# The KAN stage of a two-layer network: coefficients stationary, basis moving, output turned back by transposes

## The reference

```python
def _fourier_kan(v, coef):
    vf = v.reshape(-1, shp[-1])
    k = jnp.arange(1, GRID + 1, dtype=v.dtype)          # GRID = 8
    arg = vf[:, :, None] * k
    y = jnp.einsum('nik,jik->nj', jnp.cos(arg), coef[0]) + jnp.einsum('nik,jik->nj', jnp.sin(arg), coef[1])
```

## Time and profile before

| | us |
|---|---|
| median of three runs | 3789.62 |
| lowest, highest | 3781.47, 3795.3 |
| the profiled execution, its own time | 3786.26 |
| its span | 3784.4 |
| KAN, first xn to last statistics | 3331.21 to 3597.51 |

### The profile page before, as it was taken

One profiled execution on the slowest core, in us unless ns is written; L12 is line 12 of the kernel. 1 busy time (PEld: TensorE's weight loads), 2 busy tenths in 40 slices (PEclk: granted clock), 3 DMA queues, 4 the chain that ended last, 5 costly groups with the idle time before them and its releaser, 6 DMA issues. The chain is left out here.

```text
span 3784.4 us, 60070 instructions
## 1 busy us (share of the span) xinstructions
PE 2852.5 (75%) x18634; PEld 2068.5 (55%) x18635; DVE 2710.5 (72%) x4018; ACT 2218.7 (59%) x3974; POOL 2006.3 (53%) x1364
## 2 busy tenths in 40 slices
PE   3899999621799990378888888888888887669934
PEld 2455555321566660146666666666666666569934
DVE  3788788443344446539999999998999999867643
ACT  1566566420233330178899888898989888522242
POOL 1011111166222220169999989898989999512234
PEclk6999999655899995689999999999999999889955
DMA  3444444321111116112222222222222222120050
GB/s 95 92 89 87 83 88 90 103 73 43 39 39 39 39 34 175 30 54 74 77 80 74 78 73 73 75 77 77 77 74 77 77 80 77 58 75 25 16 156 15
DMA packets 220447, 270.13 MB, mean 71 GB/s; under 512 B 36941, under 2 KB 139879, under 8 KB 215323
## 3 DMA queue, kind: packets, MB, share of 16 engines
q1 hardware_dynamic: 199874, 247.61, 25.3%
q0 software_dynamic: 12256, 18.82, 1.5%
q10 hardware_dynamic: 8064, 0.55, 0.2%
HBM read 219.79 MB, written 54.22 MB: 72 GB/s over the span
## 5 line engine op out<-in xcount | busy, mean ns | idle before, releaser
L1740 POOL TENSOR_TENSOR resid_x<-s_ux,s_B_rows 128x1024 f32<-128x1024 f32 x256 | 605.1, 2364 | 144.1 <-PE s_y L2100 143.8
L2020 DVE TENSOR_TENSOR_SCAN resid_x<-s_dA,resid_x 128x1024 f32<-128x1024 f32 x256 | 581.6, 2272 | 127.0 <-ACT s_dA L1831 123.3
L2028 DVE TENSOR_TENSOR_SCAN resid_x<-s_back_decay,s_back_in 128x1024 f32<-128x1024 f32 x256 | 583.9, 2281 | 55.2 <-ACT s_back_decay L1841 55.2
L2100 PE MATMUL s_y<-identity,resid_x 128*128 128x128 f32 x4096 | 556.7, 281 | 18.3 <-issue 11.7
L2100 PEld LDWEIGHTS s_y<-identity,resid_x 128*128 128x128 f32 x4096 | 496.2, 146 | 71.0 <-issue 41.6
L1748 POOL TENSOR_TENSOR resid_x<-resid_x,s_C_rows 128x1024 f32<-128x1024 f32 x192 | 454.4, 2366 | 7.5 <-DVE resid_x L2020 7.5
L2087 PE MATMUL s_back_in<-identity,resid_x 128*128 128x128 f32 x2048 | 294.0, 290 | 139.4 <-ACT resid_x L1852 70.5
L467 DVE TENSOR_REDUCE a_row_max<-a_maxscores 128x2 f32<-128x512 f32 x512 | 336.0, 683 | 80.5 <-PE a_maxscores L545 80.1
L2035 DVE TENSOR_TENSOR resid_x<-resid_x,s_C 128x1024 f32<-128x1024 f32 x320 | 383.0, 1197 | 14.2 <-PE s_C L2077 10.9
L1831 ACT ACTIVATE s_dA<-s_dt,s_A 128x510 f32<-128x510 f32 x512 | 330.0, 675 | 96.3 <-DVE resid_x L2020 96.1
L1852 ACT ACTIVATE resid_x<-s_uT,s_bT 128x256 f32<-128x256 f32 x864 | 368.9, 498 | 1.3
(11 more groups left out here) (333 smaller groups left out, 5618.8 us busy)
## 6 DMA issues: line engine op xcount, KB each, us to landing
s_B_rows<-forward_rows SPq DMA_DIRECT2D x256, 256.0 KB, 3.3
s_C_rows<-forward_rows SPq DMA_DIRECT2D x192, 256.0 KB, 3.3
a_Q<-split_qk SPq DMA_DIRECT2D x96, 192.0 KB
split_qk<-a_parts SPq DMA_DIRECT2D x32, 384.0 KB, 2.8
e_x<-slot_inputs SPq DMA_DIRECT2D x135, 65.0 KB
a_K<-split_qk SPq DMA_DIRECT2D x64, 128.0 KB
f_mod_rows<-mod_rows SPq DMA_DIRECT2D x16, 512.0 KB, 9.7
c_y<-choice_outputs SPq DMA_DIRECT2D x16, 512.0 KB, 6.4
```

The source lines that it names most:

```text
L1740: tt(R[s, 0], ux[par][:], brow[s % BRING][:].unsqueeze(1).broadcast_to([P, C2, W]), ALU.mult).then_inc(S["in_ready"], 1)
L2020: nc.vector.tensor_tensor_scan(r, a, r, 0.0, ALU.mult, ALU.add).then_inc(S["scanned"], 1)
L2028: nc.vector.tensor_tensor_scan(r[:, ::-1], a[:, ::-1], b[:, ::-1], 0.0, ALU.mult, ALU.add).then_inc(S["scanned"], 1)
L2100: last = mm(YP[:, t, c2 * P:(c2 + 1) * P], R[s, d][:, c2, t * P:(t + 1) * P], core.ident[:], is_transpose=True, start=((s, d) == (0, 1) an ...
```

## The change

- The matmul is turned round. WT is stationary and the basis moves as 512 columns: 16 matmuls a group (32 instructions of 512 columns) in place of 64 (128 of 128). The output then has features on partitions. ScalarE copies it from PSUM to SBUF (`yT`), and TensorE turns it back with four transposes into a new PSUM tile `psZ`, called z below, which y1 reads.
- The nine terms that don't need ES (EARLY) are multiplied first, behind a wait for DS and EE; the seven E products (LATE) follow, behind a wait for ES. The transposes of the input of group i+1 stand between.
- xn moves from VectorE to ScalarE, with two buffers, and two groups ahead. D and E move from VectorE to ScalarE, with constants 2 and -2 as bias columns; the squares have two buffers of their own.
- The order on VectorE in turn i is now: rounding and angle of i, ES of i-1, S2 of i, y1 of i-2, DS of i, statistics of i-3.
- The hardware loops are gone: all turns of all five engines are written out. od and gate have one semaphore for each buffer.

```diff
 VectorE (constants two and minus_two are set first)
+                for i in range(NG + 4):
+                    bs, before = basis[i % 2], basis[(i + 1) % 2]
+                    if live(i):
                         dve.wait_ge(S["f_ready"], i + 1)
                         ts(whole[:], f[:], MAGIC, MAGIC, ALU.add, ALU.subtract).then_inc(S["rounded"], 1)
                         dve.wait_ge(S["rounded"], i + 1)
+                        at(dve, S["cos_done"], i)
                         tt(t[:], f[:], whole[:], ALU.subtract).then_inc(S["reduced"], 1)
+                    if live(i, 1):
+                        dve.wait_ge(S["E_ready"], i)
+                        dve.wait_ge(S["D_products"], i)
+                        tt(before[:, B_ES1:B_EDS2 + 1, :], before[:, B_S1:B_DS2 + 1, :], before[:, B_E, :].unsqueeze(1).broadcast_to([P, 7, W4]), ALU.mult)\
+                            .then_inc(S["E_products"], 1)
+                    if live(i):
                         dve.wait_ge(S["cos_done"], i + 1)
                         tt(bs[:, B_S2, :], bs[:, B_S1, :], bs[:, B_C1, :], ALU.mult).then_inc(S["s2_done"], 1)
+                    if live(i, 2):
+                        j = i - 2
+                        dve.wait_ge(S["z_ps"], j + 1)
+                        dve.wait_ge(S["hb_ready"], j + 1)
+                        at(dve, S["gated"], j)
+                        tt(y1[:], psZ[:], hb[:], ALU.add).then_inc(S["y1_ready"], 1)
+                    if live(i):
+                        dve.wait_ge(S["D_ready"], i + 1)
                         dve.wait_ge(S["s2_done"], i + 1)
                         tt(bs[:, B_DS1:B_DS2 + 1, :], bs[:, B_S1:B_S2 + 1, :], bs[:, B_D, :].unsqueeze(1).broadcast_to([P, 3, W4]), ALU.mult)\
                             .then_inc(S["D_products"], 1)
+                    if live(i, 3):
...
+                            last = tile_stats(core, X, j * KT + k)
 ScalarE
+                normed(0)
+                normed(1)
+                turns(0)
+                for i in range(NG + 2):
+                    bs = basis[i % 2]
+                    if live(i):
                         act.wait_ge(S["reduced"], i + 1)
                         at(act, S["products"], i - 1)
                         func(bs[:, B_S1, :], t[:], ACT.Sin, scale=TURN).then_inc(S["sin_done"], 1)
...
+                    if live(i, 2):
+                        j = i - 2
+                        act.wait_ge(S["products"], j + 1)
+                        at(act, S["z_ps"], j)
+                        func(yT[:], psY[:, j % 2, :], ACT.Copy).then_inc(S["yT_ready"], 1)
+                    if live(i):
                         act.wait_ge(S["sin_done"], i + 1)
+                        func(s_square[:], bs[:, B_S1, :], ACT.Square, scale=float(np.sqrt(2))).then_inc(S["q_ready"], 1)
+                        act.wait_ge(S["q_ready"], i + 1)
+                        func(bs[:, B_D, :], s_square[:], ACT.Identity, scale=-2.0, bias=two[:, 0:1]).then_inc(S["D_ready"], 1)
...
+                        func(bs[:, B_E, :], d_square[:], ACT.Identity, bias=minus_two[:, 0:1]).then_inc(S["E_ready"], 1)
...
+                    if live(i + 1):
+                        turns(i + 1)
+                    if live(i + 2):
+                        normed(i + 2)
 TensorE
+                transposes(0)
+                for i in range(NG + 2):
+                    j = i - 1
+                    product = lambda m: nc.tensor.matmul(psY[:, j % 2, :], WT[:, m, :], basis[j % 2][:, m, :], start=(m == EARLY[0]), stop=(m == LATE[-1]))
                     if live(i, 1):
+                        pe.wait_ge(S["D_products"], j + 1)
+                        pe.wait_ge(S["E_square"], j + 1)
+                        at(pe, S["yT_ready"], j - 1)
+                        for m in EARLY:
+                            product(m)
+                    if live(i + 1):
+                        transposes(i + 1)
+                    if live(i, 1):
                         pe.wait_ge(S["E_products"], j + 1)
+                        for m in LATE:
+                            last = product(m)
+                        last.then_inc(S["products"], 1)
+                    if live(i, 2):
+                        n = i - 2
+                        pe.wait_ge(S["yT_ready"], n + 1)
+                        at(pe, S["y1_ready"], n)
                         for k in range(KT):
+                            last = nc.tensor.transpose(psZ[:, k * P:(k + 1) * P], yT[:, k * P:(k + 1) * P], core.ident[:])
+                        last.then_inc(S["z_ps"], 1)
```

More of the change, by code:

```diff
@@ L2322, in kan @@
     NG, W4 = NT // KT, KT * P
-    live = lambda i, lag: not isinstance(i, int) or 0 <= i - lag < NG
+    live = lambda i, lag=0: 0 <= i - lag < NG
     on = ExitStack()
@@ L2339, in kan @@
         psY = core.psum("k_psY", [P, 2, W4], on=on)
+        psZ = core.psum("k_psZ", [P, W4], on=on)
         S = {n: core.sem("k_" + n) for n in (
-            "ln_loaded", "ln_ready", "od_loaded", "gate_loaded", "xn_ready", "xT_ps", "f_ready", "rounded", "reduced", "sin_done", "abs_done",
-            "cos_done", "q_ready", "s2_done", "D_ready", "D_products", "D_square", "E_ready", "E_products", "E_square",
-            "products", "hb_ready", "y1_ready", "gated", "x_updated", "stats", "passed")}
+            "ln_loaded", "ln_ready", "od_loaded0", "od_loaded1", "gate_loaded0", "gate_loaded1", "xn_ready", "xT_ps", "f_ready", "rounded", "reduced",
+            "sin_done", "abs_done", "cos_done", "q_ready", "s2_done", "D_ready", "D_products", "D_square", "E_ready", "E_products", "E_square",
+            "products", "yT_ready", "z_ps", "hb_ready", "y1_ready", "gated", "x_updated", "stats")}
+        EARLY = [m for m in range(NBASIS) if not B_ES1 <= m <= B_EDS2]
+        LATE = list(range(B_ES1, B_EDS2 + 1))
         with nc.Block() as block:
@@ L2365, in _ @@
                 nc.vector.memset(quarter[:], float(np.pi / 2))
+                nc.vector.memset(two[:], 2.0)
+                nc.vector.memset(minus_two[:], -2.0)
                 dve.wait_ge(S["ln_loaded"], 32)
                 ts(ln[:], ln[:], float(1 / (2 * np.pi)), None, ALU.mult).then_inc(S["ln_ready"], 1)
[L2369 to L2393, removed]
+                for i in range(NG + 4):
+                    bs, before = basis[i % 2], basis[(i + 1) % 2]
+                    if live(i):
                         dve.wait_ge(S["f_ready"], i + 1)
@@ L2408, in emit @@
[L2408 to L2413, removed]
+                    if live(i, 3):
+                        j = i - 3
+                        dve.wait_ge(S["x_updated"], j + 1)
+                        for k in range(KT):
+                            last = tile_stats(core, X, j * KT + k)
+                        last.then_inc(S["stats"], 1)
@@ L2419, in _, with normed, turns @@
                 act.wait_ge(S["ln_ready"], 1)
[L2421 to L2426, removed]
+                def normed(i):
+                    act.wait_ge(S[f"od_loaded{i % 2}"], 16 * (i // 2 + 1))
+                    at(act, S["xT_ps"], i - 1)
+                    for k in range(KT):
+                        c = i * KT + k
+                        last = func(xn[i % 2][:, k, :], od[i % 2][:, k, :], ACT.Identity, scale=core.rstd[:, c:c + 1], bias=core.nmr[:, c:c + 1])
+                    last.then_inc(S["xn_ready"], 1)
+                def turns(i):
+                    act.wait_ge(S["xT_ps"], i + 1)
+                    at(act, S["reduced"], i)
+                    func(f[:], psT[:], ACT.Identity, scale=ln[:, 0:1], bias=ln[:, 1:2]).then_inc(S["f_ready"], 1)
+                normed(0)
[4 more added lines that the diff above has]
+                    if live(i):
                         act.wait_ge(S["reduced"], i + 1)
```

72 lines of the change are left out of this document (23 added, 49 removed).

## The result

| | before | changed |
|---|---|---|
| median of four runs, us | 3791.49 | 3816.94 |
| lowest, highest | 3781.47, 3795.3 | 3813.32, 3826.05 |
| the profiled execution, its own time and span | 3786.26, 3784.4 | 3813.32, 3811.5 |
| KAN stage, first xn to last statistics | 266.3 | 296.1 |

The changed kernel is slower: the ratio is 1.0075, with a 95% interval of 1.0048 to 1.0101. The forecast said 3836 and slower; its range, 3808 to 3864, holds the measured time, but the loss is 25 us by the medians (28 by the ratio) where 47 were forecast. The profiled executions differ by 27.1 us, and the KAN stage alone by 296.1 - 266.3 = 29.8. In the runs further on, one execution of e3 took 4245.76 us, at a granted clock of 0.697 for the whole kernel where the others have 0.875 to 0.877, and is left out of e3's ratio.

A forecast was written before the change was run, and what follows sets the result against it. TensorE's stream (14.8 us a group) and the chain to ES's end (0.8 longer) were taken as bounds. Stage +33.7 us, clock +15, less 2 for ES's lateness, gave +47: 3836 us from the median 3789.6; range 3808 to 3864.

The forecast's parts named there:

- The mechanism: KAN stage turns: TensorE stands still while VectorE does y1, after z, then DS, before EARLY; 2.6 us idle a group.
- The clock: TensorE's 14 KAN-stage stalls: 0.7 of them followed by half clock, 1.5 us each, 15 us in all.
- the forecast's own sign: KAN stage's steady part: granted clock of 0.90 to 0.97 rather than 1.00, from ten falls of 3.4 us.
- The period: KAN stage, y1 to y1: 17.7 us where it was 15.6, including ES 0.2 late for LATE.
- The ends: KAN stage's two ends: first product at 3343.4, y1 of group 0 at 3374.1, last statistics' end at 3631.2.
- the 2 that ES was to give back: KAN stage: with clock falls ES is no longer late for LATE, taking 2 us off the clock's 15.
- These edits cost nothing: KAN steady state: xn, D and E on ScalarE hidden under TensorE's stream, od long landed; unrolling also at nothing.
- A: Rival, KAN stage: the same stall but the clock holds; +34 us, 3823; chance 0.13.
- E: Rival, KAN stage: part of the stall is hidden in an unseen way; +12 to +25, 3805 to 3815; chance 0.06.
- B: Rival: GpSimd's y2 gets ahead of DS, gap 1.27 us longer each time, all clocks fall; +76, 3865; chance 0.1.
- C: Rival, the 32 products: moving stream cheaper than the Mamba rows' 0.431 us spacing; -54, 3736; chance 0.03.
- D: Rival: no stall, TensorE's stream sets the pace at 14.7 to 15 us; about 3784; chance 0.08.

The follow-up runs named there:

- e3: The changed kernel with the statistics of group i-3 moved from behind DS to between y1 and DS on VectorE; ratio 1.0158 to the kernel before.
- e2: The changed kernel with the four z transposes of group i-2 moved ahead of LATE of group i-1 on TensorE; ratio 0.9941 to the kernel before.
- e4: The changed kernel's order and moved work, but products in the old direction (basis stationary, 128 columns), without yT and z; ratio 0.9957 to the kernel before.
- e7: The changed kernel run again with nothing changed, for a second profile; ratio 1.0069 to the kernel before.
- e5: e2 with xn put back on VectorE, behind ES; ratio 0.9954 to the kernel before.
- e6: The kernel before with the KAN stage's turns written out and nothing else changed; ratio 0.9994 to the kernel before.
- e1: The changed kernel with DS of group i put ahead of y1 of group i-2 on VectorE; ratio 0.9993 to the kernel before.
- e8: The changed kernel with two of the four statistics moved between y1 and DS, the other two left behind DS; ratio 1.0154 to the kernel before.

## Why the prediction was right or wrong

**The mechanism** was right in each link: z last in TensorE's turn, y1 waiting for it, DS behind y1, EARLY behind DS. Forecast idle 2.6 us, measured 2.45; forecast spacing of the products 0.431, and 28 of them in 12.18 us in e2 bear it out. That the new direction would change TensorE's own stream by next to nothing (14.65 against 14.8) was right too: e2 and e4 have 14.61 and 14.73.

**The clock** is the term that was mis-sized, and more than half of the error. The forecast put 15 us there, ten falls of 1.5, from gaps of 2.0 to 2.4 us in the Mamba stage, seven of ten of which were followed by half clock. The KAN stage had two falls, then three in e7, at 1.70 each: 3.4 to 5.1 us. The price of a fall was nearly right (1.5 against 1.70), its chance was not: by the forecast's own sign the mean granted clock was to be 0.90 to 0.97, and it is 0.99. The chance was read from a stage in which short waits stand close together: three of the ten gaps, each of 2.1 to 2.2 us, lie between 2172 and 2184 us of the kernel before, where the KAN stage has 14.9 us of unbroken work between two gaps. That this difference is the reason is argued, not shown; what is shown is that the KAN stage gives 5 in 28 at 2.45 us. The Trainium skill's "HAM oscillation" (TensorE: Matmul & The Clock Gate) describes waits of about 3 to 5 us, behind each of which the matmuls start at the low clock. The prediction had all 14 gaps fall by it, at 24 us, though they are shorter than the section's waits. At 3.79 us, a length that the section covers, 24 of 26 gaps were followed by a fall, which agrees; at 3.22 us it was 9 of 13; and at 2.45 us there are falls too, which the section doesn't tell of.

**The period** was forecast at 17.7 and is 17.32 without falls. ES was to be 0.2 late for LATE; it is ready at 3448.88 + 4.95 = 3453.83, before the 3454.21 at which LATE starts. And from the first of z's transposes to y1 it took 0.64 (forecast 0.82), from DS to EARLY 0.05 (0.13). Over thirteen periods that is 5 us.

**The ends:** first product at 3341.33 (forecast 3343.4), y1 of group 0 at 3372.53 (3374.1), from y1 of group 13 to the end 26.0 (27.0): 1.6 and 1.0, so 2.6 us less in all. With 5 for the period and 9.6 for the clock (15, less the 2 that ES was to give back, against 3.4) these make 17.2; the stage's end was forecast 46.7 later than before and came 29.4 later, 17.3 less. All three terms were too high, so none hid another. Behind the stage the changed kernel's profiled execution took 2.3 us less than before's; nothing there was changed.

**"These edits cost nothing":** borne out by e5 for xn and e6 for the loops. Moving D and E was not tested alone; e2 and e4 hold it, and both are faster than the kernel before. But the forecast's reason was wrong in one place: od is not long landed. ScalarE waits 119.6 us for it over twelve groups, mostly 9 to 9.6 us each and 13.1 at most, since its load is queued behind the gate's. In the changed kernel that is hidden: xn ends at 3451.11 + 1.65 = 3452.76, and its transposes start at 3453.77. In e1 it isn't quite.

**The rivals.** A (the clock holds, 3823) is nearer to the 3817 measured than the forecast was, and its account, the stall with hardly a fall, is nearer too: it should have had more than 0.13. But the clock did fall, two and three times; that A's figure still lies above the measured one comes from the period and the ends, which it shares with the forecast. E (part of the stall is hidden, 3805 to 3815) has the nearest figure of all, by luck: nothing of the stall is hidden, all fourteen gaps are 2.45 us. B (y2 ahead of DS, 1.27 a group) isn't what the changed kernel does, but e3 and e8 show it, at 1.34. C is out by the spacing of 0.431. D saw no support: 14.61 is reached once z is moved, and not before.

## What to carry to other kernels

When a schedule is shifted over several turns, write down for every engine what its last act of a turn releases and what its first act of the next one waits for: two engines that each end a turn with what the other needs to begin it are idle by turns, however early everything else is. A step that is only read much later belongs as early as its input allows (z, one place up, was worth 1.3%). And where a gap can make the clock fall, take the share of falls from a stretch whose gaps are as long and as far apart as those in question: the Mamba stage's seven of ten became five of 28 here, and from 2.45 to 3.79 us of gap the share went from 6 of 32 to 24 of 26.

## Unexpected in the hardware

Falls and turns can keep step. In e8 the half-clock stretches come 20.5 us apart, seven in a row and then six, with a period of 18.67 + 1.70 = 20.37:

```profile
3350.24:3353.65 3.41, 3.41 (x5) 1.37 (x5) 3.38 (x3) 0.00 (x0) 3.33 (x3) 0.50 0.32 90
3353.65:3370.72 17.07, 13.27 (x37) 6.13 (x36) 9.04 (x9) 7.78 (x14) 3.69 (x3) 1.00 0.05 16
3370.72:3374.13 3.41, 3.41 (x5) 1.35 (x4) 3.38 (x3) 2.01 (x5) 1.67 (x2) 0.50 0.21 62
```

Nearly every gap has one, while the changed kernel goes seven groups of 17.32 us between two falls (3376.4 to 3499.3). So 1.34 us more of idle time a group came with nine to eleven more falls. Whether a fall, by the 1.70 us that it adds, brings the next gap to where the clock falls again is open: no run changed the period and kept the gap.

The other is the port: DS starting 0.2 us after GpSimd's y2, and not 0.2 us before it, costs the path 1.34 us, and putting half or all of the statistics between y1 and DS makes no difference to it.
